# Second attention: the values of four quads in one block, and a ring of 32 tiles of exponentials

## The reference, cut to what matters

```python
q = (x @ wq).reshape(B, T, N_HEADS, HEAD_DIM)      # B=2, T=1024, 32 heads of 16
k = x @ wk                                         # one key and one value head for all
v = x @ wv
scores = jnp.einsum('bqhd,bkd->bhqk', q, k) * scale
scores = jnp.where(causal[None, None], scores, -jnp.inf)
probs = jax.nn.softmax(scores.astype(jnp.float32), axis=-1).astype(x.dtype)
out = jnp.einsum('bhqk,bkd->bqhd', probs, v).reshape(B, T, C)
return out @ wo
```

## Time and profile before

| | us |
|---|---|
| median of three runs (lowest, highest) | 2207.15 (2205.51, 2210.41) |
| the profiled execution's own time | 2192.01 |
| its span | 2190.2 |
| TensorE busy over the span | 2005.4 (92%) |
| VectorE busy | 1151.5 (53%) |
| ScalarE busy | 882.1 (40%) |

### The profile page before, as it was taken

One profiled execution on the slowest core, in us unless ns is written; L12 is line 12 of the kernel. 1 busy time (PEld: TensorE's weight loads), 2 busy tenths in 40 slices (PEclk: granted clock), 3 DMA queues, 4 the chain that ended last, 5 costly groups with the idle time before them and its releaser, 6 DMA issues. The chain is left out here.

```text
span 2190.2 us, 34038 instructions
## 1 busy us (share of the span) xinstructions
PE 2005.4 (92%) x12632; PEld 1155.3 (53%) x12632; DVE 1151.5 (53%) x2541; ACT 882.1 (40%) x1861; POOL 480.7 (22%) x376
## 2 busy tenths in 40 slices
PE   6858999999999999999986899997999999999698
PEld 4535665666666666666643454554444444444244
DVE  3536556555555555555401454446676666663166
ACT  3402444444444444444440122221666665665222
POOL 0011445444444444454330000000000000000000
PEclk9867999999999999999998999995999999998699
DMA  9752222233332333222336221144122223211201
GB/s 307 249 149 62 59 61 55 55 76 79 79 78 70 79 79 78 57 59 58 84 89 196 67 68 50 54 118 116 27 46 52 42 36 52 43 21 22 93 29 48
DMA packets 100856, 172.19 MB, mean 79 GB/s; under 512 B 25738, under 2 KB 46378, under 8 KB 100562
## 3 DMA queue, kind: packets, MB, share of 16 engines
q1 hardware_dynamic: 100690, 170.01, 29.4%
HBM read 84.32 MB, written 29.38 MB: 52 GB/s over the span
## 5 line engine op out<-in xcount | busy, mean ns | idle before, releaser
L839 ACT ACTIVATE at_prob<-at_scp 128x512 f32<-128x512 f32 (+1 forms) x608 | 349.2, 575 | 524.0 <-PE at_scp L940 516.1
L873 DVE CUSTOM_DVE_ANT_0 at_junk<-at_mxp,causal 128x128 f32<-128x128 f32 (+3 forms) x512 | 240.4, 485 | 344.4 <-PE at_mxp L949 339.7
L1603 ACT ACTIVATE as_prob<-as_scp 128x512 f32<-128x512 f32 (+2 forms) x640 | 309.3, 564 | 200.3 <-PE as_scp L1699 150.3
L1653 DVE TENSOR_REDUCE as_mxd<-as_mxp 128x2 f32<-128x256 f32 (+3 forms) x256 | 203.4, 820 | 97.3 <-PE as_mxp L1718 95.4
L1638 POOL TENSOR_TENSOR l_att_t<-l_att_t,as_spread 64x1024 f32<-64x1024 f32 x16 | 37.9, 2369 | 862.1 <-DMA as_spread<-l_recips 862.1
L1651 DVE TENSOR_REDUCE as_mxf<-as_mxp 128x2 f32<-128x1024 f32 x128 | 151.0, 1221 | 61.4 <-PE as_mxp L1713 61.3
L868 DVE TENSOR_REDUCE at_mxf<-at_mxp 128x1 f32<-128x512 f32 x256 | 175.6, 686 | 13.0 <-PE at_mxp L949 11.9
L782 POOL TENSOR_TENSOR at_pre<-at_prob 128x512 f32<-128x512 f32 x64 | 80.1, 1285 | 430.2 <-ACT at_prob L839 430.2
L782 POOL TENSOR_TENSOR at_pre<-at_pre,at_prob 128x512 f32<-128x512 f32 x128 | 160.4, 1283 | 3.6 <-ACT at_prob L839 0.8
L1737 PE MATMUL as_op<-as_prob,l_vn 128*32 128x512 f32 (+3 forms) x1536 | 160.7, 541 | 0.5 <-ACT as_u_sb L1610 0.5
L949 PE MATMUL at_mxp<-l_khi,hd_early_q 96*128 96x512 f32 (+2 forms) x384 | 135.3, 421 | 23.3 <-DMA hd_early_q<-at_shi 21.1
(11 more groups left out here) (226 smaller groups left out, 3371.0 us busy)
## 6 DMA issues: line engine op xcount, KB each, us to landing
hd_early_q<-at_shi SPq DMA_DIRECT2D x96, 128.0 KB, 2.4
hd_late_q<-at_slo SPq DMA_DIRECT2D x96, 128.0 KB, 2.4
at_qhi<-at_shi SPq DMA_DIRECT2D x96, 128.0 KB, 2.4
at_qlo<-at_slo SPq DMA_DIRECT2D x96, 128.0 KB, 2.4
at_spread<-l_recips SPq DMA_DIRECT2D x64, 128.0 KB, 2.8
l_o<-at_u_sb SPq DMA_DIRECT2D x16, 512.0 KB, 4.2
hd_early<-in_wmod SPq DMA_DIRECT2D x7, 1024.0 KB, 5.7
hd_late<-l_o SPq DMA_DIRECT2D x12, 512.0 KB, 4.4
```

Source lines behind the costliest of these rows:

```text
L839: nc.scalar.activation(prob[:, x % RING0, c0:HALF], scp[x % BANKS0][:, c0:HALF], ACT.Exp).then_inc(s["exp_done"], 1)
L873: nc.vector.tensor_tensor_reduce(out=junk[:, u % 2, 0:w], in0=tile[:, 0:w], in1=k.causal[:, HALF - w:HALF], scale=1.0, scalar=LOWEST, op0= ...
L1603: nc.scalar.activation(prob[:, x % RING1, cols], scp[x % BANKS1][:, cols], ACT.Exp).then_inc(s["exp_done"], 1)
L1653: nc.vector.reduce_max(mxd[:, t % 2, :, i, qt:qt + 1], tile[:, :, 0:(qt % 4 + 1) * P], AX_X).then_inc(s["mx_done"], 1)
```

## The change

Where TensorE did the values of two quads behind every second quad, it does those of four quads behind every fourth: behind quad g with g mod 4 = 1, from 5 on, it takes quads g - 5 to g - 2. As a step has twelve quads, this is always behind quads 1, 5 and 9, and the blocks hold quads 8 to 11 of the step before, 0 to 3, and 4 to 7. The ring has 32 tiles where it had 24. No instruction is added or removed.

```diff
-MXBANKS, BANKS1, RING1 = 2, 3, 24
+MXBANKS, BANKS1, RING1, TOGETHER = 2, 3, 32, 4
...
                         for j in range(2 * i, min(2 * i + 2, UNITS1_OF[n])):
                             score(t, n, j)
-                    if g % 2 and g >= 3:
-                        values(*divmod(g - 3, QUADS))
-                        values(*divmod(g - 2, QUADS))
-                for g in (QSETS - 2, QSETS - 1):
+                    if g % TOGETHER == 1 and g > TOGETHER:
+                        for i in range(g - 1 - TOGETHER, g - 1):
+                            values(*divmod(i, QUADS))
+                for g in range(QSETS - TOGETHER, QSETS):
                     values(*divmod(g, QUADS))
```

## The result

The changed kernel takes 2249.5 us (median of four runs, 2238.4 to 2265.1) beside 2206.3 for the kernel before: a ratio of 1.0215, with a 95% interval of 1.0135 to 1.0294. It is slower, as forecast, but by 43 us where 13 were forecast and 26 were the end of the range. The profiled execution took 2265.1 us, 73.1 more than that of before: of these, some 30 are that the profiled execution of before lay 14 us under its median and this one 16 above.

What follows compares the result with a forecast made beforehand. TensorE was taken as the bound on average, with VectorE and ScalarE holding it up in stretches. Removed blocks 8.3, last quads 1 and clock 4 made 13 us slower, from 2207 to 2220 us; range 2200 to 2233.

Steps and rivals of the forecast that it cites:

- The direction and the bound: Second attention: slower; TensorE the bound on average, but VectorE and ScalarE run dry in blocks and hold TensorE up in stretches.
- the walk through the banks: Stretches after each removed block: time gained against work moved, given PSUM bank waits; 0.6 us a step, 8.3 us slower.
- The three removed blocks: Blocks behind quads 3, 7 and 11: -0.02, +0.3 and -0.87 us a step, 8.3 us slower in all.
- The border of 0.15 us: Each block on TensorE costs 0.15 us of border; 47 fewer would gain 7 us if TensorE were the bound throughout.
- rule of the drain: A change of tiling mode between scores and values drains TensorE; by it alone the change would gain 7 us.
- sentence on interleaved regimes: Interleaving may help where the most-contended engine changes over time; the change interleaves less, so should cost; no size given.
- The last 16 quads: Quads without maxima at the end, where three blocks go: 1 us lost, between 1.8 lost and 0.4 gained.
- The readings: Profile readings of the second attention, such as ScalarE waiting 150 us for scores and quad 8's exponentials following at 1608.4.
- The clock: Falls from 2.4 to 1.2 GHz, 1.65 us each: 4 us lost, between 13 lost and 10 gained.
- The ring: Ring of exponentials at 32 tiles: costs nothing, as each overwritten tile's quad was already taken by an earlier block.
- The TensorE-bound case: Rival: waits inside stretches are mostly pipeline, so borders count; 7 us faster, 2200 us; chance 15% together with a no-falls variant.
- The case of a clock that falls in every step: Rival: long stretches of quads 6 to 9 are thin for TensorE; 22 us slower, 2229 us; chance 25%.

Runs made afterwards that it cites:

- one_copies: Kernel before with a block of one quad's values behind every quad, and the copies out of the bank one quad earlier; 2184.7 us, ratio 0.9876.
- join7: Kernel before with only the block behind quad 7 taken away, quads 4 to 7 together behind quad 9, ring 24; 2228.8 us, ratio 1.0084.
- half_four: Changed kernel with half of each long maximum left out and exponentials of 0.05 times the score, output wrong; 2219.6 us, ratio 1.0048 to before.
- four_ring24: Changed kernel's order of values with the old ring of 24 tiles; 2241.8 us, ratio 1.0154 to the kernel before.

## Why the prediction was wrong, step by step

**The direction and the bound** were right. The stage has two regimes, and a block is cover for the other engines as well as work. But of the 43 us only 7 come from the walk through the banks that carried the forecast; the rest is the clock, which was held to be the smaller term. That the time rose so clearly is luck, and no merit of that sum.

**The three removed blocks.** Forecast -0.02, +0.3 and -0.87 us a step, measured by the stretches at full clock: that of quads 2 to 5 is 7.42 and replaces 3.40 + 3.87 + 0.15, so 0.00; that of 6 to 9 is 8.67 for 4.34 + 4.44 + 0.15, 0.26 gained; that of 10 to 1 is 7.90 for 3.05 + 3.95 + 0.15, 0.75 lost. The sum is 0.5 a step, 7 us in all, against 8.3.

**The border of 0.15 us** was right: the new blocks measure 2.29 and 3.57 us, which is the moved matmuls and one border less each. The Trainium skill's rule of the drain (TensorEngine Tiling, Key Properties) fits a real cost, though no run separates the drain from the rest of a border; in this kernel that cost is the smaller one. The Trainium skill's sentence on interleaved regimes (Perfetto Trace Analysis, Optimization Strategy) pointed the right way, and one_copies, which goes further in its direction, is the faster for it.

**The last 16 quads**: forecast 1 us; from the last maximum to the last values both profiled executions take 49.6 us, with 24 and 25 of them at the lower clock. Nothing was lost there.

**The readings** hold but for two small ones that change nothing: ScalarE's 150 us are its waits for L1699 alone, with 47 more for L1696, and the earlier trace rows let quad 8's exponentials follow at 1608.5 to 1608.6 rather than 1608.4.

**The clock** is the step that failed. The prediction named it as the open cost, priced one fall at 1.65 us, counted at most one a step, and took 4 us with 13 as the end. Measured: 597.1 - 523.6 = 73.5 us in the profiled execution, of which 7 are the steps; 66 are left for 178 us more at the lower clock, 0.37 us for each. By the medians it is 43 in all, so some 36 for the clock. The number of falls and the length of each were both too small. I took one fall a step because only one place had one before, although I had just written that the stretches without values become longer, and there are three of them in a step. And I took each fall to last 3.4 us, though in the new kernel most last 6.8 or 10.2. (The price of a microsecond at the lower clock, 1.65 / 3.41 = 0.48, was if anything too high: it is that of a block, and a part of the new falls lies in stretches.) The reason given for 4 us, that the stretch of 6 and 7 stays as it is, was wrong as well: without the block behind quad 7 it runs on through quads 8 and 9, and in join7 this one stretch lost clock in 11 of 14 steps.

A part of the evidence was at hand: every one of the six falls started at the end of the one stretch in which TensorE waited for both others, and lay in the block behind it. The bound should have been the long stretches and the blocks behind them at half speed. The stretches alone are not enough: join7's takes 11.4 us for 8.7, 2.7 lost, while a step with such a fall takes 36.8 for 31.4, 5.5 lost, the other half in the blocks.

**The ring** at nothing was wrong too, by about 10 us. No exponential waits for a tile, as the prediction says; the cost shows in the time at the lower clock, and what links the two is not known.

**The rivals.** The TensorE-bound case (2200 us) is refuted by the stretches and by one_copies. The case of a clock that falls in every step (2229) had the right mechanism, but priced it at 13 us where some 36 were measured.

## What to carry to other kernels

Where two kinds of matmul take turns on TensorE, ask not only who waits for a bank, but whether a stretch of the thinner kind gets long. Short turns mostly kept the clock and gave the other engines cover, and that was worth more than the borders saved (31.15 us a step with twelve blocks and the copies moved, 31.63 with six, 32.14 with three, all at full clock). If a profile has even a few falls of the granted clock, all at one kind of place, a change that makes such places longer or more numerous is to be bounded by the whole of them, and of the work right behind them, at half speed. And compare steps at full clock first: they tell the order's effect to some 0.05 us, while the medians carry the clock's.

## What the runs showed of the hardware that I had not expected

- TensorE lost its clock while it was busy for 90% and more of the time: in half_four's stretch of quads 6 to 9 its busy time is 9.85 of 10.60 us at a granted clock of 0.69. The busy share did not foretell where: in the changed kernel the stretch of 6 to 9, busy for 8.33 of 8.67 us at full clock, lost clock in 9 of 14 steps, and that of 10 to 1, busy for 6.81 of 7.90, in 6.
- A fall outlasted the stretch in which it began. Of the 29 falls of the changed kernel between its first values and its last maximum, 28 began in a stretch, and about half of the low time lay in blocks.
- 178 us more at half the clock cost 66 us, not 89. A block lost 0.48 us for each at the lower clock (4.42 for 2.29), and join7's stretch of quads 6 to 9 only 0.24 (11.40 for 8.67), where at full clock TensorE waits for the others. The pair four_ring24 and before gives 42.3 us for 106, of which 7 are the order's: 0.33 for each.
- Useless matmuls over all rows raised the stage's granted clock from 0.84 to 0.93 and the kernel's speed by 0.5%. Whether any matmul would do, or only those over all 128 rows, was not tried.
- The number of tiles in a ring in memory, from 24 to 32, with no instruction added and no exponential waiting for a tile in either, moved the time by 5.6 us in one order and 10 us in the other.
